# A transformer block on one core: the second sequence's input in front of the last weight pieces, q ahead of k in the first sequence, and the projection in two halves

## The reference, cut to what matters

```python
h = layernorm(layernorm(x)) -> q, k, v = h @ qkv_w + qkv_b     # 16 heads of 16 channels
attn = softmax(q k / 4 over a window of 15 tokens) @ v
x1 = layernorm(x) + attn @ proj_w + proj_b
x2 = x + x1 + gelu(layernorm(x1) @ fc1_w + fc1_b) @ fc2_w + fc2_b
z = layernorm(x2)
main = gelu(z @ W1m + b1m) @ W2m + b2m                         # 256 -> 1024 -> 256
two experts of eight, chosen by softmax(mean(z) @ w_gate + b_gate), same shape
out = x2 + a * main + (1 - a) * (gate_0 * expert_0 + gate_1 * expert_1)
```

## Time and profile before

| what | value |
|---|---|
| median of 3 runs | 2013.59 us (2012.11 to 2015.28) |
| the profiled execution | 2011.87 us, of which its span 2010.1 us |
| PE busy | 1980.8 us (99% of the span) |
| DVE, ACT, POOL busy | 73%, 56%, 46% |
| mean granted TensorE clock | 0.998 |
| chain that ended last | PE 92%, DVE 4%, issue 2% |

### The profile page before, as it was taken

The page is one execution under the profiler, slowest core; times in us unless marked ns, Lnnn a source line. Parts: engine busy times, 40 slices in busy tenths (PEclk is TensorE's granted clock), DMA queues, the critical chain, the costliest instruction groups (busy, mean ns, idle before and its releaser), DMA issues.

```text
span 2010.1 us, 37531 instructions
## 1 busy us (share of the span) xinstructions
PE 1980.8 (99%) x13454; PEld 1813.9 (90%) x13454; DVE 1475.0 (73%) x2462; ACT 1135.5 (56%) x1801; POOL 928.1 (46%) x909
## 2 busy tenths in 40 slices
PE   7899999999999999999999999999999999999999
PEld 6789999999999999999999999999999999999998
DVE  8687786867868687786877868678686776868753
ACT  5465555646556565565555556455565655655554
POOL 6436155362543635245361553625436353453625
PEclk9999999999999999999999999999999999999999
DMA  3121110212102121121211102121021211212121
GB/s 111 43 64 53 52 50 27 74 54 58 53 28 73 43 74 43 45 56 37 75 53 50 51 27 74 53 58 52 29 71 45 74 44 41 60 38 74 43 59 53
DMA packets 188848, 108.79 MB, mean 54 GB/s; under 512 B 65436, under 2 KB 187640, under 8 KB 188664
## 3 DMA queue, kind: packets, MB, share of 16 engines
q1 hardware_dynamic: 187316, 105.43, 18.5%
q10 hardware_dynamic: 1348, 0.98, 0.2%
HBM read 85.52 MB, written 8.39 MB: 47 GB/s over the span
## 4 chain that ended last, share of the span: by engine, by line
PE 92%; DVE 4%; issue 2%; ACT 1%; POOL 1%; DMA 0%; ACTq 0%; POOLq 0%; DVEq 0%
PE psB L233 50%; PE psA L233 25%; PE psA L1082 5%; PE psA L1109 5%; PE psA L1094 3%; PE psA L1001 2%; DVE pr L622 1%; DVE smax L618 1%; DVE acc L560 1%; POOL wm_lo L425 0%; DVE hr_lo L544 0%; POOL wf_lo L425 0%; PE psA L1126 0%; DVE rinv L620 0%; DMA raw<-in_L_attn_qkv_w 0%
## 5 line engine op out<-in xcount | busy, mean ns | idle before, releaser
L544 DVE TENSOR_TENSOR hr_lo<-hf,hr_hi 128x512 fp32r<-128x512 f32 x512 | 494.4, 966 | 427.8 <-ACT hr_hi L851 427.3
L851 ACT ACTIVATE hr_hi<-hf 128x512 fp32r<-128x512 f32 x512 | 323.8, 632 | 273.0 <-PE psB L233 184.8
L436 POOL TENSOR_TENSOR wx_lo<-raw,wx_hi 128x512 fp32r<-128x512 f32 x256 | 396.7, 1549 | 21.4
L434 POOL TENSOR_SCALAR wx_hi<-raw 128x512 fp32r<-128x512 f32 x256 | 186.4, 728 | 357.3 <-PE psB L233 343.3
L847 ACT ACTIVATE hf<-psB,b1x 128x512 f32<-128x512 f32 x256 | 175.1, 684 | 199.4 <-PE psB L233 198.4
L233 PE MATMUL psB<-wx_hi,hr_hi 128*128 128x256 f32 x1024 | 287.5, 281 | 0.2
L233 PE MATMUL psB<-wx_hi,hr_lo 128*128 128x256 f32 x1024 | 286.3, 280 | 0.0
L233 PE MATMUL psB<-wx_lo,hr_hi 128*128 128x256 f32 x1024 | 285.7, 279 | 0.0
L450 POOL TENSOR_SCALAR kb<-kT 64x384 f32<-64x384 f32 x128 | 81.3, 635 | 357.5 <-ACT kT L867 349.6
L233 PE MATMUL psB<-z_hi,wx_hi 128*128 128x512 f32 x512 | 210.9, 412 | 0.0
L233 PE MATMUL psB<-z_hi,wx_lo 128*128 128x512 f32 x512 | 202.5, 395 | 0.0
(11 more groups left out here) (153 smaller groups left out, 5126.8 us busy)
## 6 DMA issues: line engine op xcount, KB each, us to landing
raw<-in_L_ffn_W1e SPq DMA_DIRECT2D x256, 128.0 KB, 2.2
raw<-in_L_ffn_W2e SPq DMA_DIRECT2D x256, 128.0 KB, 2.2
out_x<-acc SPq DMA_DIRECT2D x32, 256.0 KB, 2.2
xin<-in_L_attn_x SPq DMA_DIRECT2D x15, 512.0 KB, 3.8
vb<-vs SPq DMA_DIRECT2D x64, 96.0 KB
vb<-vs SPq DMA_DIRECT2D x62, 80.0 KB
tm<-in_L_ffn_b2e SPq DMA_DIRECT2D x32, 128.0 KB, 3.0
raw<-in_L_attn_fc_w SPq DMA_DIRECT2D x8, 256.0 KB, 4.1
```

The costliest lines, as they stand in the source:

```text
L434: g.tensor_scalar(wx[0][:, s, :], raw[:, s, :], 1.0, 0.0, ALU.mult, ALU.add).then_inc(w_hi.sem, 1)
L436: g.tensor_tensor(wx[1][:, s, :], raw[:, s, :], wx[0][:, s, :].bitcast(f32), ALU.subtract).then_inc(w_lo.sem, 1)
L544: v.tensor_tensor(hr[1][:, c % 2, :], hf[:, c % 3, :], hr[0][:, c % 2, :].bitcast(f32), ALU.subtract).then_inc(h_lo.sem, 1)
L851: a.activation(hr[0][:, c % 2, :], hf[:, c % 3, :], ACT.Copy).then_inc(h_hi.sem, 1)
```

## The change: what it does

- SP loads pieces up to 16 first, then the second sequence's `xin`, then pieces 17 to 20. POOL makes the low parts of pieces 17 to 20 only after the second sequence's normalised tiles are written (`z1_s`).
- On POOL the roots of the first layernorm stand in front of the constants `hmask` and `band`; the second set of roots stands behind them. The zeroing of `vb` moves behind `keys(0, 0)`.
- In sequence 0 q is projected before k, and into bank 3; the first values go to bank 2. The waits follow: the first scores wait for `kT` and no longer for the first values or for ACT's half of q.
- In all sequences `project` is cut by halves of the input channels: 12 matmuls for k = 0 at q = 13 and 12 for k = 1 at q = 14, accumulated in banks 0 and 1 instead of 2 and 3.
- In sequence 0 the 12 filler matmuls at q = 12 go, and 5 come at q = 13.

```diff
             windows(sp, 0, range(4))
-            weights(2 * RING, NPC)
+            weights(2 * RING, 17)
...
                         sp.dma_start(xin[:, :, :], x[t + 1, :, :].rearrange("(i p) n -> p i n", p=P)).then_inc(xload.sem, 16)
+                        if t == 0:
+                            weights(17, NPC)
...
-            assert made == N_CONST, made
-            for j, (a_, b_) in ((1, EXTRA[1]), (0, EXTRA[0])):
+            def roots(j, a_, b_):
...
-            g.memset(vb[:, :, :, :, :], 0.0).then_inc(zeroed.sem, 1)
+
+            roots(1, *EXTRA[1])
+            const(g.memset(hmask[:, :], 1.0))
...
+            const(g.memset(band[:, :], 0.0))
...
+            assert made == N_CONST, made
+            roots(0, *EXTRA[0])
...
             keys(0, 0)
+            g.memset(vb[:, :, :, :, :], 0.0).then_inc(zeroed.sem, 1)
             weights(4, 8)
...
                     elif q == SPLIT + 5 and t == 0:
+                        g.wait_ge(z1_s.sem, z1_s.all(1))
                         weights(17, NPC)
...
-                v.wait_ge(qk.sem, qk.at(t, 2 * c + 1))
+                v.wait_ge(qk.sem, qk.at(t, 2 * c + 1 if c or t else 0))
...
-                src = psA[:, 3 if c else 1, th * UB * QB:(th + 1) * UB * QB].rearrange("p (b q) -> p b q", q=QB)
+                src = psA[:, 3 if c or t == 0 else 1, th * UB * QB:(th + 1) * UB * QB].rearrange("p (b q) -> p b q", q=QB)
...
-                v.tensor_tensor(vs[:, 2 * n:2 * n + 2, :], psA[:, 2 if n else 0, :].rearrange("p (i n) -> p i n", n=D),
+                v.tensor_tensor(vs[:, 2 * n:2 * n + 2, :], psA[:, 2 if n or t == 0 else 0, :].rearrange("p (i n) -> p i n", n=D),
...
-                    v.tensor_tensor(sl, sl, psA[:, 2 + h, :], ALU.add).then_inc(x1.sem, 1)
+                    v.tensor_tensor(sl, sl, psA[:, h, :], ALU.add).then_inc(x1.sem, 1)
...
-                a.wait_ge(qk.sem, qk.at(t, 2 * c))
+                a.wait_ge(qk.sem, qk.at(t, 2 * c if c or t else 1))
...
-                bank = 2 if n else 0
+                bank = 2 if n or t == 0 else 0
...
                 for h in range(2):
-                    if u == 0 and h == 0:
+                    if u == 0 and t == 0:
+                        pe.wait_ge(kT_s.sem, kT_s.at(0, 0))
+                    elif u == 0 and h == 0:
                         pe.wait_ge(vs_s.sem, vs_s.at(t, 0))
...
-            def project(t):
-                pe.wait_ge(tA_lo.sem, tA_lo.all(t))
-                pe.wait_ge(aT_s.sem, aT_s.all(t))
+            def project(t, k):
+                pe.wait_ge(tA_lo.sem, tA_lo.at(t, k))
                 for h in range(2):
+                    if k == 0:
+                        pe.wait_ge(pT_s.sem, pT_s.at(t, 6 + h))
                     for j in range(2):
                         i = 2 * h + j
-                        for k in range(KD):
-                            last = three(pe, psA[:, 2 + h, j * D:(j + 1) * D], [z[:, k, LEFT + i * P:LEFT + (i + 1) * P] for z in zT],
-                                         [w[:, k, :] for w in wproj], k == 0, k == KD - 1)
-                    last.then_inc(proj.sem, 1)
+                        last = three(pe, psA[:, h, j * D:(j + 1) * D], [z[:, k, LEFT + i * P:LEFT + (i + 1) * P] for z in zT],
+                                     [w[:, k, :] for w in wproj], k == 0 and j == 0, k == KD - 1 and j == 1)
+                    if k == KD - 1:
+                        last.then_inc(proj.sem, 1)
...
-            WARM = {1: 10, 3: 2, 4: 4, 8: 8, 9: 8, 10: 3, 11: 4, 12: 12, 14: 12, 16: 8}
+            WARM = {1: 10, 3: 2, 4: 4, 8: 8, 9: 8, 10: 3, 11: 4, 13: 5, 14: 12, 16: 8}
...
+            project_qk(0, 0, 0, 3)
             project_qk(0, 0, 1, 0)
-            project_qk(0, 0, 0, 1)
             pe.wait_ge(rows_in.sem, rows_in.all(0))
-            pe.wait_ge(kT_s.sem, kT_s.at(0, 0))
             values(0, 0)
...
                         if t:
                             pe.wait_ge(z3_lo.sem, z3_lo.at(t - 1, 0))
+                        else:
+                            pe.wait_ge(vs_s.sem, vs_s.at(0, 0))
                         values(t, 1)
...
                     elif q == 3:
                         if t:
                             pe.wait_ge(z3_lo.sem, z3_lo.all(t - 1))
+                        else:
+                            pe.wait_ge(qm_odd.sem, qm_odd.at(0, 3))
                         project_qk(t, 1, 0, 3)
...
+                    elif q == 13:
+                        project(t, 0)
                     elif q == 14:
-                        project(t)
+                        project(t, 1)
                     elif q == 16:
                         pe.wait_ge(z_s.sem, z_s.at(t, NT - 1))
                         for c in range(KD):
-                            pe.wait_ge(pT_s.sem, pT_s.at(t, 6 + c))
+                            pe.wait_ge(x1.sem, x1.at(t, c))
                             transposes(tr2, c, tm, c)
```

More of the change, by code:

```diff
@@ L366, in _ @@
                                   pattern=[[-1, P]], channel_multiplier=1))
[L368 to L372, removed]
             def power(row, n, adds, tiles=range(NT)):
@@ L415, in _ @@
                     g.tensor_tensor(rs[:, j * NT + lo:j * NT + hi], ve[:, j * NT + lo:j * NT + hi], mhalf[:, 0:hi - lo], ALU.pow).then_inc(rstd_first.sem, 1)
-            g.memset(vb[:, :, :, :, :], 0.0).then_inc(zeroed.sem, 1)
+            roots(1, *EXTRA[1])
+            const(g.memset(hmask[:, :], 1.0))
+            for h in range(2):
+                v = hmask[64 * h:64 * h + 64, :]
+                const(g.affine_select(out=v, in_=v, compare_op=ALU.is_ge, fill=0.0, base=0, pattern=[[-HD, HS]], channel_multiplier=1))
+                const(g.affine_select(out=v, in_=v, compare_op=ALU.is_ge, fill=0.0, base=HD - 1, pattern=[[HD, HS]], channel_multiplier=-1))
+            const(g.memset(band[:, :], 0.0))
+            for h in range(HS):
+                v = band[QB * h:QB * h + QB, :]
+                const(g.affine_select(out=v, in_=v, compare_op=ALU.is_ge, fill=-1e30, base=RAD - LEFT, pattern=[[1, KW]], channel_multiplier=-1))
+                const(g.affine_select(out=v, in_=v, compare_op=ALU.is_ge, fill=-1e30, base=LEFT + RAD, pattern=[[-1, KW]], channel_multiplier=1))
+            assert made == N_CONST, made
+            roots(0, *EXTRA[0])
             g.wait_ge(dzero.sem, 7)
```

## The result

The changed kernel takes 2047.18 us (median of 4 runs, 2046.23 to 2048.33), the kernel before 2013.26 (2012.11 to 2015.28): a ratio of 1.0168, 95% interval 1.0153 to 1.0183. It is slower by 33.9 us; 13 were forecast. The direction and one of the two places were right, the size was not.

The account below looks back on a forecast made before the run. From the second sequence on, PE's work plus every wait it is given was taken to bound the kernel. +19.5 us in sequences 1 to 15 and -5.8 in sequence 0 gave +13.7, so 2026.4 us, range 2019 to 2034.

Parts of the forecast that it names:

- The tiles' wait, 15 x 1.3: Sequences 1 to 15: PE's transposes wait 1.3 us each for norm2_apply's late tiles, +19.5 us in all (18.6 to 21.0).
- The rest of the loop is unchanged, so PE doesn't get it back: Sequences 1 to 15, behind the transposes: the new wait of 1.3 us stays in the time in full.
- Sequence 0, -5.8: Sequence 0 and the start of 1: the edits there gain 5.8 us together, between -8.3 and +0.0.
- the wait of 3.61: Second sequence's input: PE's wait for the normalised tiles goes; with part given back, -3.2 us (-4.5 to -0.9).
- the second half's first mask: Sign in sequence 0: DVE's first mask of the second half should stand near 21.5 instead of 23.38.
- the 0.7 that was forecast for the halves: Sequence 0: the first sum comes after six matmuls instead of twelve, -0.7 us (0 to -0.8).
- at 1.38 each: Start of sequence 1: POOL's four low parts fall on two zT_lo subtractions, giving back at most 1.38 us each.
- What starts earlier ends earlier: Sequence 0, q first: DVE has no idle until all four blocks are normalised, so earlier scores gain 1.9 us.
- The tiles didn't escape POOL: Rival, sequences 1 to 15: tiles run ahead of POOL's split, PE does not wait, 2006 to 2007.8 us; chance fully 0.10, half 0.05.
- The zeroing began at 19.39: Rival, sequence 0: DVE's scaling of b2main is stuck behind POOL's zeroing of vb; 3.6 less gain, 2030.0 us; chance 0.05.
- cost no clock: Rival: the clock falls at each new wait, transposes cost 0.9 more per sequence, 13.5 on top, 2039.9 us; chance 0.03.
- the edits of sequence 0 do nothing: Rival: nothing is gained in sequence 0, so +19.5 us stands alone, 2032.2 us; chance 0.03.

Follow-up runs that it names:

- Kernel 12: Changed kernel, but POOL begins split 10 of the expert weights only after hr_lo of chunk 16 in sequences 1 to 15: 2034.04 us, ratio 1.0126.
- kernels 6: Changed kernel with the whole projection at q = 14 in sequences 1 to 15, and there the third unit's query blocks before hr_lo of chunk 4: 2006.74 us.
- 10: Kernel before the change, with only the third unit's query blocks moved ahead of hr_lo of chunk 4 in sequences 1 to 15: 2006.16 us, ratio 0.9983.
- kernels 1: Changed kernel, but the projection whole again at q = 14 in sequences 1 to 15, still in banks 0 and 1: 2009.54 us, ratio 1.0002.
- 2: Kernel before the change, plus only the projection in halves (banks 0 and 1) in sequences 1 to 15: 2043.68 us, ratio 1.0170.
- 9: Changed kernel, but POOL holds only the low part of split 9 until the normalised tiles are written, sequences 1 to 15: 2029.33 us, ratio 1.0097.
- 3: Changed kernel, but in sequences 1 to 15 DVE does gather before scaling and splitting the second layernorm's transposed tiles: 2036.01 us, ratio 1.0135.
- 4: Changed kernel, but POOL holds all of split 9 until the four normalised tiles are written, sequences 1 to 15: 2043.54 us, ratio 1.0169.
- 5: Changed kernel, but both projection halves stand behind chunk_down(12) in sequences 1 to 15, first channel first: 2036.77 us, ratio 1.0134.

## Why the prediction was wrong, by its own steps

**The tiles' wait, 15 x 1.3: right.** Its whole chain came as written: `hr_hi` at 670.04 and so 1.0 us ahead of the projection's last matmul (671.07) instead of 2.4, the first sum straight behind `hr_lo`, tr2 late by 1.24, once in each sequence. 15 x 1.24 = 18.6, where 19.5 was forecast.

**"The rest of the loop is unchanged, so PE doesn't get it back": the step that failed.** It asked only whether PE could gain time behind the transposes, not what else would be late there. The sum lacked a term of 15 x 1.02 = 15.3. The chain was followed on DVE up to the last tile and no further; behind it in DVE's queue stood two `hr_lo`, the transposed tiles and `gather`, and for `gather` PE waits. And only one of POOL's splits was looked at. Split 9 moved along with the tiles, as the prediction said; split 10 did not. It had been paced by PE, and with POOL late it came in one piece with split 9, on top of the two `hr_lo`. The gap of 0.63 us in POOL's row at 668.80, the length of the two `hr_lo` and the start of `gather`, 3.85 behind tr2, stood in the trace of before and were not read. Kernel 12 shows the cause: with split 10 held back, 0.76 of the 1.02 go.

**Sequence 0, -5.8: wrong, it is 0 within some 3 us (kernels 6 and 10).** The single gains came: the wait of 3.61 went, and the second half's first mask stood at 20.29 (21.5 was forecast; all of sequence 0 began about 1 us earlier in this run, because the fourth weight piece landed earlier: ACT's table load behind it ran at 8.81 instead of 9.80). From the projection that waits for the second channel half to tr2 it is 6.35 us instead of 7.04, the 0.7 that was forecast for the halves. All this was given back in two places, and behind the wait of 3.53 by the clock as well, a cost that the prediction did not weigh there. That POOL's low parts would meet the `zT_lo` subtractions was in the range, at 1.38 each; they cost 3.01 of wait, less 0.37 before. That the fourth mask, at 37.65 instead of 41.34, would bring the subtraction behind it onto POOL's bias sum was not seen. "What starts earlier ends earlier" holds only as long as what runs beside it stays the same.

**The account.** Of the two profiled executions (2047.84 after, 2011.87 before, 36.0 apart): A 18.6, B 15.3 and C 15 x 0.37 = 5.5, together 39.4 (38.9 by the mean of 14 sequences), less 2.9 to 3.4 in sequence 0 and the start, of which 1.0 is the weight piece that landed earlier. The medians lie 33.9 apart, 2 us less; C differs between kernels that are alike there, so it may differ between runs of one kernel too, which no run here shows directly: in kernels 1, 2 and 9, whose profiled run has the long C, that run lies 3.4 to 5.2 us above the median, in 3, 4, 5 and 12 at most 1.7. So the stretches name the places better than the price. Against the changed kernel, 15 times the table's stretches are 14.6 us less in kernel 9, where the ratios give 14.3, but 11.4 to 15.3 less in 3, 5 and 12, where the ratios give 6.6 to 8.4. The cost of the halves is taken from kernel 2, which has nothing else: 34.6 us.

**The rivals.** The tiles didn't escape POOL (2.07 for two, as before). The zeroing began at 19.39, after DVE had scaled the constant at 18.57, and the subtraction beside it, at 21.87, took its usual 0.96. The mean granted clock was 1.00 from 112 us to the end, so in sequences 1 to 15 the new waits of 1.03 and 0.74 cost no clock; in sequence 0 it fell with the longer one of 3.53. That the edits of sequence 0 do nothing was given 0.03. Its number is what the runs show, though not its reason: the edits gained and gave it back.

**What stays open.** Which edit turns the collision at the query blocks to the side of DVE: kernels 1, 2 and 9 have it turned, 3, 4, 5 and 12 not, with and without the halves.

## What to carry to other kernels

When a step is made late, follow each engine's queue past the first wait, until every engine is back at its old distance; here the second wait cost nearly as much as the first, and came in full for half the lateness. An engine that waits for the bottleneck is paced by it; make it late for another reason and its work comes in one piece, on top of what it used to alternate with. And before work is moved earlier, look at what the other engine does at the new time: the three edits that paid here move no matmul. Two keep DVE's and POOL's work apart, and one lets DVE do first what PE waits for.

## What the runs showed of the hardware

In these traces two-input DVE operations and POOL operations that read shut each other out, and which of the two pays turns on hundredths of a microsecond. The subtraction of the fourth mask and POOL's bias sum met in both kernels. Before, DVE and then POOL:

```profile
43.49 0.96 DVE L613 TENSOR_TENSOR pr<-pr,smax 128x768 f32<-128x768 f32 x1
```

```profile
43.53 3.19 POOL L456 TENSOR_TENSOR y<-y,bproj 128x1024 f32<-128x1024 f32 x1
```

DVE was first by 0.04 and POOL paid 0.8 (3.19 against 2.41). After, POOL was first by 0.02 (39.66 and 39.68) and DVE paid 2.24. The Trainium skill says on the page "SBUF — State Buffer", section "Who interferes with whom", that a DVE instruction with two SBUF inputs contends with a GpSimd instruction that reads SBUF, and that the order of issue decides which of the two blocks. The traces agree. The price of losing is most of the other's instruction, 2.24 of POOL's 2.41 us and 0.8 of DVE's 0.96, so a long POOL operation beside short DVE ones is a risk of its own, and one that a change anywhere ahead of it can call due.
